# The order of the first loads in a quantized linear layer behind a conditioned mix, and the high part of tile 0 on one engine

## The reference

```python
x: (64, 64, 1024) float32        condition: (64,) of 0..15
W = weights[condition]           # weights: (16, 64, 64)
y = einsum('bct,bcd->bdt', x, W) # mix of the 64 channels, by condition
# qweight: (1024, 768) int32; of each three words, four values of 6 bits
v0 = p[:, :, 0] & 63;  v1 = p[:, :, 0] >> 6 & 63
v2 = p[:, :, 1] & 63;  v3 = p[:, :, 2] & 63
w = (unpacked - zero_point) * scale             # (1024, 1024)
out = x + einsum('bsk,nk->bsn', y, w) + bias
```

## Time and profile before

| | us |
|---|---|
| median of 3 runs (lowest, highest) | 285.9 (285.17, 285.96) |
| the profiled execution | 285.48 |
| its span, first to last instruction | 283.7 |
| TensorE busy in the span | 276.7 (98%) |
| VectorE, ScalarE, GpSimd busy | 191.9, 84.0, 99.2 |

### The profile page before, as it was taken

The page is one execution under the profiler, slowest core; times in us unless marked ns, Lnnn a source line. Parts: engine busy times, 40 slices in busy tenths (PEclk is TensorE's granted clock), DMA queues, the critical chain, the costliest instruction groups (busy, mean ns, idle before and its releaser), DMA issues.

```text
span 283.7 us, 8491 instructions
## 1 busy us (share of the span) xinstructions
PE 276.7 (98%) x3307; PEld 231.1 (81%) x3307; DVE 191.9 (68%) x261; ACT 84.0 (30%) x170; POOL 99.2 (35%) x41
## 2 busy tenths in 40 slices
PE   6999999999999999999999999999999999999995
PEld 2878887788888887988888888888888888888885
DVE  2898897785566556865559555676667655595554
ACT  3785334332044300633017310443106330060000
POOL 4005903964430444314442444404443044430000
PEclk9999999999999999999999999999999999999999
DMA  7930563446115541355113551145413562101112
GB/s 280 373 117 16 175 229 126 154 158 230 74 74 157 174 168 71 113 158 194 74 74 124 161 214 74 74 155 157 156 68 109 168 209 88 74 37 74 74 74 75
DMA packets 20278, 37.96 MB, mean 134 GB/s; under 512 B 6814, under 2 KB 7070, under 8 KB 20266
## 3 DMA queue, kind: packets, MB, share of 16 engines
q1 hardware_dynamic: 19322, 35.43, 36.3%
q10 hardware_dynamic: 944, 2.38, 2.2%
HBM read 21.02 MB, written 16.78 MB: 133 GB/s over the span
## 4 chain that ended last, share of the span: by engine, by line
PE 96%; DMA 2%; issue 1%; ACT 0%; DVE 0%; SPq 0%
PE o_ps L297 71%; PE y_ps L297 12%; PE y_ps L266 10%; DMA w_sb<-in_L_cond_weights_dram 1%; PE o_ps L266 1%; PE o_ps L279 0%; DMA ids<-in_itok_B_dram 0%; PE y_ps L279 0%; PE o_ps L308 0%; PE y_ps L308 0%; ACT y_hi L434 0%; ACT qT L457 0%; SPq L164 0%; DVE o_sb L638 0%; DVE o_sb L640 0%
## 5 line engine op out<-in xcount | busy, mean ns | idle before, releaser
L297 PE MATMUL o_ps<-qT,y_hi 128*128 128x512 f32 (+1 forms) x448 | 171.5, 386 | 0.2 <-ACT qT L457 0.2
L297 PE MATMUL o_ps<-qT,y_lo 128*128 128x512 f32 (+1 forms) x448 | 171.2, 385 | 0.0
L660 POOL TENSOR_TENSOR resid<-x_sb,bias_bc 128x1024 f32<-128x1024 f32 x32 | 95.8, 3002 | 151.0 <-DVE o_sb L563 130.7
L297 PEld LDWEIGHTS o_ps<-qT,y_hi 128*128 128x128 f32 x448 | 83.6, 188 | 17.4 <-issue 0.6
L297 PEld LDWEIGHTS o_ps<-qT,y_lo 128*128 128x128 f32 x448 | 83.6, 188 | 17.0
L555 DVE TENSOR_TENSOR o_sb<-o_ps,scale_bc 128x512 f32<-128x512 f32 x54 | 37.4, 692 | 73.4 <-PE o_ps L297 73.4
L434 ACT ACTIVATE y_hi<-y_ps 128x512 fp32r<-128x512 f32 x56 | 29.4, 610 | 96.8 <-PE y_ps L266 96.4
L563 DVE TENSOR_TENSOR o_sb<-o_sb,resid 128x512 f32<-128x512 f32 x63 | 51.5, 823 | 1.9
L425 ACT ACTIVATE junk<-x_sb 128x1024 bf16<-128x1024 f32 x32 | 33.8, 1058 | 63.6 <-DMA x_sb<-in_x_dram 63.6
L544 DVE SCALAR_TENSOR_TENSOR resid<-zs_bc,ysum,resid 128x1024 f32<-128x1024 f32 x32 | 44.9, 1405 | 0.0
L534 DVE TENSOR_TENSOR y_lo<-y_ps,y_hi 128x512 fp32r<-128x512 f32 x57 | 35.7, 688 | 5.4 <-ACT y_hi L434 5.4
(11 more groups left out here) (45 smaller groups left out, 69.8 us busy)
## 6 DMA issues: line engine op xcount, KB each, us to landing
x_sb<-in_x_dram SPq DMA_DIRECT2D x32, 512.0 KB, 3.4
out_dram<-o_sb SPq DMA_DIRECT2D x63, 256.0 KB, 2.1
q_raw<-in_L_ffn_qweight_dram ACTq DMA_DIRECT2D x6, 384.0 KB, 5.7
w_sb<-in_L_cond_weights_dram SPq DMA_DIRECT2D x63, 16.0 KB, 2.0
q_raw<-in_L_ffn_qweight_dram SPq DMA_DIRECT2D x2, 384.0 KB, 7.2
out_dram<-o_sb SPq DMA_DIRECT2D x2, 128.0 KB, 1.9
ids<-in_itok_B_dram SPq DMA_DIRECT2D x1, 0.2 KB
w_sb<-in_L_cond_weights_dram ACTq DMA_DIRECT2D x1, 16.0 KB, 3.6
```

The lines of the kernel that those rows point to most:

```text
L297: last = nc.tensor.matmul(bank, part[:, slot, kt, :], qT[:, kt, col:col + width], start=(kt == 0 and part is y_hi), stop=(kt == KT - 1 and ...
L660: nc.gpsimd.tensor_tensor(resid[:, j % RING, :], x_sb[:, j % RING, :], bias_bc[:], ALU.add).then_inc(xbias_ready, 1)
```

## The change

SyncE issues the first weight half of tile 1 ahead of tile 1's rows and the second one behind them; of the blocks it issues 6 and 7, no longer 4 and 6. ScalarE issues block 0 only ahead of tile 0's second weight half, and blocks 1 to 5 behind it. ScalarE copies both halves of tile 0's high part, one after the other, ahead of block 1's placing; VectorE's copy is gone, and its low part waits for each half by itself. The two warm-up matmuls between the transposes of block 0 and the mix of tile 0 are gone.

```diff
@@ SyncE
             load_w_half(sp, 0, 0, pick_first(sp, 0))
+            load_w_half(sp, 1, 0, pick_first(sp, 2))
             load_x(1, 0)
-            for half in range(2):
-                load_w_half(sp, 1, half, pick_first(sp, 2 + half))
-            for n in (4, 6):
+            load_w_half(sp, 1, 1, pick_first(sp, 3))
+            for n in (6, 7):
                 load_q(sp, n)
@@ TensorE
             transpose_q(0)
-            keep_warm(2)
             wait_mix(0, 0)
             mix(0, y_banks[0])
@@ ScalarE
-            def high(j, i, banks, halves=range(2)):
+            def high(j, i, banks):
                 t = i * RING + j
-                for half in halves:
+                for half in range(2):
@@ ScalarE
-            for n in range(2):
-                load_q(act, n)
+            load_q(act, 0)
             act.wait_ge(warm_ready, 1)
             nc.scalar.activation(junk[:, 1, 0:1], warm[:, 0:1], ACT.Copy)
             act.wait_ge(ids_loaded, 16)
             load_w_half(act, 0, 1, pick_first(act, 1))
-            for n in (2, 3, 5, 7):
+            for n in range(1, 6):
                 load_q(act, n)
             place_q(0)
-            high(0, 0, y_banks[0], range(1))
+            high(0, 0, y_banks[0])
             place_q_halves(1)
@@ VectorE
-            def low(j, i, banks, whole=False):
+            def low(j, i, banks):
                 t = i * RING + j
-                if whole:
-                    dve.wait_ge(y_hi_ready, t * 2 + 2)
                 for half in range(2):
-                    if not whole:
-                        dve.wait_ge(y_hi_ready, t * 2 + half + 1)
+                    dve.wait_ge(y_hi_ready, t * 2 + half + 1)
@@ VectorE
             for n in range(3):
                 unpack_q(n)
-            dve.wait_ge(y_ps_ready, 2)
-            nc.vector.tensor_copy(y_hi[:, 0, :, S:2 * S], y_banks[0][1]).then_inc(y_hi_ready, 1)
-            low(0, 0, y_banks[0], whole=True)
+            low(0, 0, y_banks[0])
             unpack_q(3)
```

## The result

The changed kernel takes 287.52 us (median of six runs, 286.91 to 288.4) against 285.71 for the kernel before on the same chip (285.14 to 285.96): ratio 1.0067, 95% interval 1.0049 to 1.0086, 1.8 us slower. The profiled execution took 287.19, its span is 285.4. The prediction was 285.7 with a range up to 286.9: wrong.

The account below looks back on a forecast made before the run. TensorE was taken to bound the kernel (96% of the span), so only its first dense start at 9.33 counted. A gain of 0.18, rounded to -0.2, on the median 285.9 gave 285.7 us, range 284.9 to 286.9.

Parts of the forecast that it names:

- rival B: Tile 0's weights land no earlier (fixed delay, not bytes); first product at 9.85, +0.5, 286.4; chance 0.11.
- Rival C: Block 1 lands at 6.0, block 2 at 7.0; first product near 8.7, time 285.3 or 285.1; chance 0.12.
- rival E: TensorE's 1.17 us gap without a releaser at 49.06 moves, by up to 1.2 either way; chance 0.05.
- Step 6: Behind the first quarter: later blocks, tile 1's second weight half, rows and later tiles change nothing, 0; slack 0.35.
- Step 4: Block 1, issued behind the weights at 3.20 instead of 1.15, lands at 6.50 instead of 6.42, no bubble.
- rival A: Tile 1's rows go before block 2; first product 1.1 later, 287.0, or 286.65 with equal shares; chance 0.18.
- step 5: Block 2 against tile 1's rows: block 2 lands at 7.6, first product starts at 9.15, gain 0.18.
- Rival D: TensorE's clock falls to 1.2 GHz between 5.0 and 9.33, up to +3, 289; chance 0.02.

Follow-up runs that it names:

- the last experiment: Kernel before, with blocks 2 to 5 on ScalarE's queue, 6 and 7 on SyncE's, and tile 1's first weight half ahead of its rows: 285.71 us (0.999).
- the first four experiments: Changed kernel with: blocks 4 and 6 back on SyncE, 286.64; tile 1's weights behind rows, 286.67; both, 287.93; blocks 6 and 7 held until block 5 lands, 289.48.

## Why the prediction was wrong

Right: that TensorE's first dense moment, not the loop, carries the difference; that the weights land earlier and the mix with them (5.91 forecast, 5.69 measured), so rival B did not happen; that this is worth next to nothing at the first product, as blocks 1 and 2 hold it (9.15 forecast, 9.50 measured, released by a transpose and not by ScalarE); that the high part on ScalarE is covered in the changed kernel. Rival C (earlier blocks) did not happen either, and the gap of rival E is 1.03 instead of 1.17. The high part and the missing warm-ups together cost nothing that can be measured as long as block 1 is in front.

**Step 6 is the step that failed, and it carried the loss.** I priced all that follows the first quarter at zero: block 4's wait as hidden, tile 1's second half as keeping its place, and the rest by "the same total of bytes". Block 3, which must be unpacked when the first quarter ends, was not costed at all, nor was block 5. Block 3 landed at 11.9 (4.32 and 7.6; 9.9 before) and cost 1.38; block 5 landed at 15.9 and cost 0.48. Block 4, forecast about a microsecond earlier, landed at 13.2 (4.94 and 8.3), 0.4 later than before. The total of bytes says when the last load lands, not which one lands late.

For block 3 the runs show the reason: with block 1 behind the weights it no longer gets through ahead of tile 1's rows. For block 5 they show it in part. With blocks 6 and 7 held back it came 2.3 us earlier, but with block 1 in front and 6 and 7 beside it (the last experiment) it was issued at 4.95 and landed 7.7 later, at 12.6, in time. So the two beside it are not enough to make it late.

The Trainium skill (DMA: Bandwidth & Descriptors, "Issuing engines are not separate DMA queues") says that DMAs from different engines interleave. In the changed kernel the trace agrees: block 6, issued at 5.80 on SyncE's queue, took 8.6 and landed at 14.4, ahead of block 5 on ScalarE's, issued at 5.42 and landed at 15.9. I weighed the rule against one pair of loads, found it contradicted there, and used it for block 2 alone.

**Step 4 left out the cause.** I costed the landing of block 1 by bytes and found no bubble, and for block 1 the number came out (6.5 forecast, unpacked from 6.62). I asked only when block 1 would land, not what its move does to the loads around it: 0.34 MB less moved by 9, and one block less ahead of the rows. Block 2 (7.6 forecast) was unpacked from 8.03, 0.4 late; the wait of 0.42 is over the 0.3 that I had named as the sign of rival A, yet the rows landed at 11.8, so the sign misleads. Putting block 1 back, and nothing else, brings back 385 GB/s and the time of the kernel before, and moving it alone on the kernel before costs 1.2 us or more; that makes its place the root. By which mechanism packets take longer with it behind the weights is not shown.

Smaller slips: step 5 put the issue of the rows at 3.9, it was 4.22. Of the chances, the forecast, B and half of A alone add up to 0.72, so 0.73 leaves nearly nothing for "most of C"; nothing rests on it.

**Rival A** had the right kind of event at the wrong place: tile 1's rows get ahead of a block that is needed sooner. It happens at block 2 with block 1 behind the weights and the rows issued at 3.25, and costs 1.2 to 1.3 there in the time of two runs at full clock; in the changed kernel the rows are issued at 4.22, block 2 lands before them and block 3 with them.

**Rival D** was given 2 in 100. In the changed kernel it holds for one of six runs. In the three kernels with gaps of 1.7 to 2.0 us in the opening the mean clock was under 0.998 in four of seven, five of eight and five of eleven runs; those with 0.992 or 0.994 took 1.2 to 2.4 us more than their faster twins. Of the kernel before, timed beside all of these, three of 89 runs had such a clock.

The parts don't add up one by one: at full clock the changed kernel is 1.7 above the one before, the split or the weight order taken back leaves 0.8 each, both taken back 0.6, and both, alone or together, on the kernel before cost nothing. They cost only with block 1 behind the weights. With three to ten runs each, and runs of one kernel up to 1.9 apart at full clock, 0.6 and 0.8 can't be told apart. Why the fifth block on ScalarE's queue takes 10.5 us in the changed kernel, and 9.7, 9.5, 8.3 and 8.1 in the first four experiments, I have not settled.

## What to carry to other kernels

When a load is moved back in a queue, ask for every later load that something waits for, one by one, when it lands now, what runs on the other queue beside it, and how much slack its reader has; "the same bytes" answers only for the last. Ask above all which load now falls behind a big one of the other queue: here that was one block, 2.0 us later. In these kernels block 1 was also worth issuing early for the rate: with it behind the weights 319 to 350 GB/s were moved from 2 to 9, with it in front 382 to 393. An earlier start of a stage whose next input is not earlier is worth nothing, and the kernels with a gap of 1.7 to 2.0 us in TensorE's opening ran at a lowered clock in 14 of 26 runs. And one profile is one execution: between kernels with the same loads in the same order block 1 was unpacked from 6.7 to 8.2, so a difference of that size needs more than one profile before it is given a cause.

## What the runs showed of the hardware

Two things I had not expected. After a gap of 2.02 us in TensorE's work the granted clock was 0.50 from 10 to 12; the runs of that kernel with a mean clock of 0.994 took 1.4 to 2.3 us more than the median of their twins at full clock. With the gap of 1.74 filled by eight matmuls on zeros no run of six was lowered. And with a DMA share of 1.02 the engines moved 298 GB/s, against 377 at 0.96: a full share doesn't say that bytes flow at full rate. Part of this is small packets (176 under 512 B against 11), but over the 7 us from 2 to 9, with 313 against 268 of them, it is still 337 GB/s at 0.96 against 385 at 1.01.
